# Cross-attention and mixture of experts on one core: the mixture by units of 256 rows, with the weights as stationary operand

## The reference, cut to what matters

```python
router_probs = softmax(layernorm(x) @ gate_w)          # E = 8 experts
topk_w, topk_idx = top_k(router_probs, 2)               # TOP_K = 2, weights made to sum to 1
h = silu(rows @ w1[e]) * (rows @ w3[e])                 # M = 896
out = h @ w2[e]                                         # back to D = 256
x = x + sum over the two experts of topk_w * out
```

## Time and profile before

| | us |
|---|---|
| median of the runs (462.66 to 465.39, three runs) | 465.23 |
| the profiled execution, its own time | 464.74 |
| its span | 463.0 |
| TensorE products busy (3921) | 428.7 |
| ScalarE busy | 230.9 |
| GpSimd busy | 213.3 |
| VectorE busy | 209.6 |

### The profile page before, as it was taken

How to read it: one execution, slowest core, us unless ns; L and a number is a source line. 1 busy time by engine, 2 the same in 40 slices (tenths; PEclk the granted TensorE clock), 3 DMA queues, 4 the chain that set the end, 5 groups by cost and what they waited for, 6 DMA issues and landing times.

```text
span 463.0 us, 12218 instructions
## 1 busy us (share of the span) xinstructions
PE 428.7 (93%) x3921; PEld 396.0 (86%) x3922; DVE 209.6 (45%) x582; ACT 230.9 (50%) x477; POOL 213.3 (46%) x209
## 2 busy tenths in 40 slices
PE   3899999999999999989999998999999999999970
PEld 3789988898988888979999898899999899999970
DVE  4457788758876784323233331333232333233220
ACT  3677777578865523745333732553272373333320
POOL 4424375657434641798321671482177177121121
PEclk9999999999999999999999999899999999999996
DMA  8644121462128448335731236118121121121121
GB/s 255 195 134 156 47 70 48 145 234 70 49 59 286 114 128 260 80 122 168 256 54 24 37 110 187 23 35 272 23 43 29 23 39 30 23 46 23 36 37 11
DMA packets 34523, 46.10 MB, mean 100 GB/s; under 512 B 3488, under 2 KB 29344, under 8 KB 34464
## 3 DMA queue, kind: packets, MB, share of 16 engines
q1 hardware_dynamic: 22304, 31.82, 20.6%
q0 software_dynamic: 6576, 8.82, 11.3%
q10 hardware_dynamic: 5584, 4.76, 3.7%
HBM read 32.63 MB, written 12.76 MB: 98 GB/s over the span
## 4 chain that ended last, share of the span: by engine, by line
PE 68%; DVE 9%; issue 6%; POOL 5%; DMA 4%; ACT 2%; ACTq 1%; POOLq 1%; DVEq 0%
PE bank L814 28%; PE twin L833 15%; PE bank L852 4%; DMA out_rows<-qf,x_all 3%; POOL w_lo L486 3%; PE twin L667 3%; PE bank L547 3%; PE bank L548 2%; PE bank L549 2%; DVE w_lo L1229 2%; PE bank L593 2%; PE twin L679 2%; PE bank L571 2%; PE twin L792 1%; PE bank L610 1%
## 5 line engine op out<-in xcount | busy, mean ns | idle before, releaser
L496 POOL DMA_INDIRECT out_rows<-qf,x_all x35 | 54.6, 1559 | 147.4 <-ACT qf L1054 111.7
L814 PE MATMUL bank<-w_hi,c_hi 128*128 (+1 forms) x280 | 106.4, 380 | 3.8 <-issue 2.0
L814 PE MATMUL bank<-w_lo,c_hi 128*128 (+1 forms) x280 | 103.0, 368 | 0.0
L833 PE MATMUL twin<-w_hi,kv_halves 128*128 (+1 forms) x490 | 95.2, 286 | 2.9 <-DVE kv_halves L1335 2.4
L1329 DVE TENSOR_TENSOR x_all<-bank,x_all 128x448 f32<-128x448 f32 x70 | 43.4, 623 | 97.3 <-ACT x_all L1073 97.2
L486 POOL TENSOR_TENSOR w_lo<-raw,w_hi x18 | 76.0, 4422 | 12.8 <-ACT w_hi L1066 10.1
L1335 DVE TENSOR_TENSOR kv_halves<-bank,kv_halves 128x512 fp32r<-128x512 f32 x66 | 38.6, 623 | 93.9 <-ACT kv_halves L1078 93.9
L833 PEld LDWEIGHTS twin<-w_hi,kv_halves 128*128 128x128 f32 x490 | 77.5, 188 | 3.7 <-DVE kv_halves L1335 2.6
L814 PE MATMUL bank<-w_hi,c_lo 128*128 (+1 forms) x280 | 79.9, 367 | 0.0
L1073 ACT ACTIVATE x_all<-bank 128x448 f32<-128x448 f32 x70 | 37.8, 544 | 80.6 <-PE bank L814 70.1
L833 PE MATMUL twin<-w_lo,kv_halves 128*128 (+1 forms) x245 | 68.7, 280 | 0.0
(11 more groups left out here) (219 smaller groups left out, 703.4 us busy)
## 6 DMA issues: line engine op xcount, KB each, us to landing
raw<-in_w SPq DMA_DIRECT2D x24, 896.0 KB
x_all<-bucket ACTq DMA_DIRECT2D x31, 129.0 KB, 2.1
raw<-in_ctxT SPq DMA_DIRECT2D x8, 256.0 KB, 2.9
out_rows<-x_all SPq DMA_DIRECT2D x8, 256.0 KB, 2.1
bucket<-pad_rows SPq DMA_DIRECT2D x13, 129.0 KB, 2.4
x_all<-in_x SPq DMA_DIRECT2D x2, 512.0 KB, 6.4
x_all<-bucket SPq DMA_DIRECT2D x6, 129.0 KB, 2.7
x_all<-in_x SPq DMA_DIRECT2D x1, 768.0 KB, 6.3
```

What stands on the lines that cost most here:

```text
L496: pool.indirect_dma_start(out=out, out_offset=bass.IndirectOffsetOnAxis(ap=x_in[:, v, D:D + 1].bitcast(U32), axis=0), in_=y[:, v, :], in_o ...
L814: last = nc.tensor.matmul(bank[b][:, 0:MC], stationary[:, k, :], w[:, bass.ds(at + (of + k * M + c * MC), MC)], start=(k == 0 and part == ...
L833: last = nc.tensor.matmul(bank[6][:, 0:D], stationary[:, k, :], w[:, bass.ds(at + (2 * W13 + k * D), D)], start=(k == 0 and part == 0 and ...
```

## The change

Constants: units of TWO = 256 rows instead of tiles of 128; EARLY holds two units (expert 1's and expert 0's first two tiles); a unit's last or only odd tile is a "single". The lists count units.

TensorE. The gate and up products (`gate_up`) go by blocks c of 128 of the 896 hidden columns. The weights are the stationary operand, and x, transposed, moves: 256 columns are the 256 rows of a unit. The result has the hidden columns on the partitions, as the down product needs it, so there are no transposes of g. For a single tile, x's high and low halves (`c_halves`, 2 times 128 columns) move together, and VectorE adds up the two halves of the result (`sums`); the result of low weights by low x is thereby in the sum as well.

```diff
-            def hidden(t, c):
-                for k in range(KD):
-                    for part, stationary in enumerate((x_hi, x_lo)):
-                        for b, of in ((c, 0), (2 + c, W13)):
-                            for w in ((w_hi, w_lo) if part == 0 else (w_hi,)):
-                                last = nc.tensor.matmul(bank[b][:, 0:MC], stationary[:, k, :],
-                                                        w[:, bass.ds(at + (of + k * M + c * MC), MC)], ...
+            def gate_up(t, e, c, single=False):
+                if c == 0:
+                    pe.wait_ge(x_hi_ready, t + 1)
+                    pe.wait_ge(w13_ready, e + 1)
+                if single:
+                    pe.wait_ge(summed, MB * t + max(c - 1, 0))
+                for i in range(2):
+                    if single:
+                        for k in range(KD):
+                            for w in (w_hi, w_lo):
+                                last = nc.tensor.matmul(out_ap, block(w, k), c_halves[:, :, k, 0:P], ...
+                        continue
+                    for k in range(KD):
+                        nc.tensor.matmul(out_ap, block(w_hi, k), x_hi[:, k, :], start=(k == 0), stop=False)
+                        nc.tensor.matmul(out_ap, block(w_lo, k), x_hi[:, k, :], start=False, stop=False)
+                    for k in range(KD):
+                        last = nc.tensor.matmul(out_ap, block(w_hi, k), x_lo[:, k, :], ...
+                last.then_inc(h_done, 1)
+            def down(t, c, at, tiles=2):
+                pe.wait_ge(g_lo_ready, MB * t + (c + 1))
+                for o in range(tiles):
+                    (three products: g_hi, g_lo stationary, 256 columns of w2 moving)
+            def unit(t, e, at_before, single=False):
+                gate_up(t, e, 0, single)
+                gate_up(t, e, 1, single)
+                down(t - 1, MB - 1, at_before)
+                gate_up(t, e, 2, single)
+                gate_up(t, e, 3, single)
+                first_down(t, e, tiles)
+                gate_up(t, e, 4, single)
+                down(t, 1, at, tiles)
+                x_transposes(t + 1)
+                gate_up(t, e, 5, single)
+                down(t, 2, at, tiles)
+                gate_up(t, e, 6, single)
+                for c in (3, 4, 5):
+                    down(t, c, at, tiles)
```

The early order on TensorE interleaves units 0 and 1 with the rest of the attention: rank(NPR - 1) stands behind gate_up(1, e1, 2); behind it gate_up of blocks 3 to 6 and down of blocks 0 to 4 of unit 1, then x_transposes(2), down of block 5 and the wait for six tables of the list. After that the experts are written out one by one:

```diff
+            for e in range(E):
+                of = e * NT + (3 if e < 2 else 1)
+                start = pe.value_load(tab_start[0:1, e:e + 1], ...)
+                def pairs_if_listed(j):
+                    with pe.If(pe.value_load(tab_pairs[0:1, of + 2 * j:of + 2 * j + 1], ...)):
+                        unit(start + j, e, ...)
+                        if j == 0:
+                            pairs_if_listed(1)
+                        else:
+                            with pe.If(pe.value_load(tab_pairs[0:1, of + 4:of + 5], ...)):
+                                with pe.Fori(2, NT // 2 - (1 if e < 2 else 0)) as r:
+                                    with pe.If(pe.value_load(tab_pairs[0:1, bass.ds(2 * r + of, 1)], ...)):
+                                        unit(start + r, e, e % 2 * WALL)
+                pairs_if_listed(0)
+                with pe.If(pe.value_load(tab_odd[0:1, e:e + 1], ...)):
+                    t = pe.value_load(tab_single_at[0:1, e:e + 1], ...)
+                    before_it = pe.value_load(tab_expert[0:1, bass.ds(t - 1, 1)], ...)
+                    unit(t, e, pe.snap((before_it % 2) * WALL), single=True)
```

ScalarE, VectorE and GpSimd go through the units unrolled, with tests only behind unit SURE = 16 (an untaken test leaves the whole chain of units):

```diff
+        def units_of_mixture(eng, step):
+            for t in range(AHEAD, SURE):
+                step(t)
+            def unit_if_used(t):
+                go = eng.value_load(tab_active[0:1, t:t + 1], ...)
+                with eng.If(go):
+                    step(t)
+                    if t + 1 < MOST - 2:
+                        unit_if_used(t + 1)
+            unit_if_used(SURE)
 # ScalarE
+            def silus(t, c):      (256 columns of bank c % 4, after h_done, and after summed)
+            def high_g(t, c):     (256 columns, bank to g_hi, after g_ready)
+            def mix(t):
+                high_halves(first, t, 0)
+                block_of(t, 0)
+                block_of(t, 1)
+                evacuate_y(t - 1, ...)          (two instructions of 256 columns)
+                high_halves(first, t, 1)
+                block_of(t, 2)
+                block_of(t, 3)
+                high_halves(first, t, 2)
+                block_of(t, 4)
+                block_of(t, 5)
+                evacuate_x(t + 1)               (512 columns)
+                block_of(t, 6)
+                copy_meta(t + 1)                (token numbers and weights, ring of four)
+                load(t + 2)                     (two row numbers, two DMAs)
 # VectorE
+            def products(t, c, n=TWO):  (up half of the bank times silu, back into the bank)
+            def low_g(t, c, n=TWO):
+            def sums(t, c):             (singles: 512 columns of a bank to 256, before the silu)
+            def mix(t):
+                (reads opening, single and double from the tables, three branches)
+                with dve.If(opening):
+                    for c in range(MB):
+                        if c == MB - 1:
+                            split_x(t + 1)
+                        products(t, c); low_g(t, c)
+                        if 1 <= c:
+                            low_halves(e, at, (c - 1,))
```

So the low halves of the next expert are made by VectorE, one piece of 896 columns behind each of blocks 1 to 6 of an expert's first unit (behind all blocks where the first unit is a single), and no longer by GpSimd; `w13_ready` and `w2_ready` take the place of `expert_ready`. GpSimd only adds: two adds for each unit, each after the one before, also for the empty second tile of a single:

```diff
-            def low_part(at, i):
-                return pool.tensor_tensor(w_lo[:, bass.ds(at + i * W13, W13)], ...
+            def mix(t):
+                for o in range(2):
+                    add_unit(t - 1, o)
 ...
-            pool.wait_ge(x2_stored[0], 16 * 7)
-            add(0, 0)
             scatter(NPR - 2)
             scatter(NPR - 1)
-            add(1, 1)
-            add(2, 2)
+            pool.wait_ge(x2_stored[0], 16 * 7)
+            for o in range(2):
+                add_unit(0, o)
```

More of the change, by code:

```diff
@@ L902, in _ @@
+            n = units_used(pe)
+            down(n - 1, MB - 1, (E - 1) % 2 * WALL)
         @block.scalar
@@ L1057, in high_halves @@
+            def high_halves(first, t, part):
                 if first is None:
```

676 lines of the change are left out of this document (359 added, 317 removed).

## The result

The changed kernel takes 535.35 us (median of six runs, 534.87 to 536.88), against 466.45 us for the kernel before on the same chip: a ratio of 1.150 (95% interval 1.1445 to 1.155). The forecast was 487, with a range of 464 to 505. The direction was right; the size was too small by 48 us.

What follows compares the result with a forecast made beforehand. The prediction took TensorE, busy 93% of the span, as the bound. To 464.7 us it added 11 for the first stretch, 3.5 for the middle and 7.5 for the end: 486.7, say 487, range 464 to 505 (forecast band 475 to 497).

Steps and rivals of the forecast that it cites:

- The products: TensorE's matmul work: 0.1176 us a product, 15.3 us a pair, 9.5 a single; -18.9 us in all, the only sure term.
- First stretch: Up to the start of unit 2: the longer list on VectorE delays it from 176.4 to 187, +11 us.
- The tests on TensorE: Middle stretch: loads, tests and empty rounds on TensorE's sequencer stop the array for 18.4 us, bounds 8 to 30.
- rival B: TensorE's jumps: seven untaken branches over more than one unit each fetch code, 2.65 us each, +18.6, 505 us; chance 0.22.
- The clock: Middle stretch: one wait as long as expert 2's brings TensorE a stretch at half clock, losing 1.7 us.
- The openings: Six units that prepare the next expert's weights: ScalarE's work of 18.0 us exceeds TensorE's 15.3; 3 us each, 18 in all.
- The double counting: Middle stretch: 5 us taken off for lateness of other engines made up during a test on TensorE.
- The register loads of ScalarE: Opening units: register loads, tests and DMA issues counted as 2.8 us within ScalarE's 18.0 us of work.
- The end: After the last product: two adds in a row, 4.8 us, and ScalarE's exit jump, 2.7 us; +7.5.
- Rival A: Middle stretch: waits at the handover between ScalarE, VectorE and TensorE do not appear, the work gained shows; 450 us, chance 0.16.

Runs made afterwards that it cites:

- e8_no_list: Changed kernel with every engine's order of units and the row numbers as constants, low halves on GpSimd, list of units not made: 457.14 us, ratio 0.981.
- e14_stops: e8_no_list with ten register loads in a row on TensorE ahead of the first unit of experts 2 to 7: 502.27 us, ratio 1.065.
- e4_gpsimd_low: Changed kernel with the next expert's low halves moved from VectorE back to GpSimd, in three pieces: 518.11 us, ratio 1.113.
- e1_listed: Changed kernel with TensorE's order of units as constants, no register loads or branches there; other engines keep theirs: 510.77 us, ratio 1.0965.
- e3_thin: e1_listed with the openings' pieces of the next expert's halves cut from 896 to 64 columns on ScalarE and VectorE: 478.03 us, ratio 1.028.
- e10_act_listed: Changed kernel with TensorE's and ScalarE's order of units as constants and low halves on GpSimd; VectorE and GpSimd keep their tests: 479.42 us, ratio 1.021.
- e2_short_jumps: Changed kernel with TensorE's order of units as constants but as many tests, no branch passing over a unit's code: 524.56 us, ratio 1.128.

## Why the prediction was wrong

**The products.** Right. 0.118 us each and 15.41 us for a unit without waits, against 15.3; 14 pairs and 3 singles of 9.5 make 244 us, against 242.7. The step that was called the only sure term was sure.

**First stretch.** Forecast +11, measured +13.8. The twelfth table of the list was written at 178.8 and the second x tile landed at 181.7, as the chain said (178.4 and 181.4); x's halves were complete at 184.2. TensorE's sequencer began its loads and tests at 181.8 and needed 8.4 us: 4.4 as forecast (4.3), and 4.03 for the branch at 183.6 over expert 0's pairs, which the forecast had at nothing. e8_no_list shows that the list, with the loads of row numbers, was worth 9.5 us of the time.

**The tests on TensorE, and rival B.** The loads, tests and five empty rounds were put at 18.4 us, and the far branches at nothing. From start to start of products, less the 0.118 of a product, the ten stops of the middle are 34.9 us; 14.4 of that are far branches, five of the six (the sixth lies ahead of unit 2). This was the step that failed most. I took TensorE's branch back over eight tiles (0.26 us) as the price of all its branches; six forward jumps took 2.4 to 4.0 us, because they waited for code. Rival B had the mechanism and nearly the sum, 7 x 2.65 = 18.6 us against 18.4 for six, but the sum is luck. Of the seven branches that it named only the two of experts 0 and 1 were long. The five at the third pair pass over one copy of a pair, not over more than one unit as the prediction says, and took 0.33 us each; the other four long ones are tests for a single, each close behind another jump, and the prediction did not count them. The Trainium skill ("Runtime: NRT & Kernel Launch", Instruction fetch mechanics) says that a branch out of the resident window forces a fetch; the trace agrees for the six long branches, each of which ends 1.3 to 1.4 us after a packet of q8, and a single jump over one unit's code (0.33 us, L911) did not wait for one. The prices of the loads held: the rest of the stops is 20.5 us against 18.4. (Two of that sum's items do not follow from its own 0.93 a test, 10.2 should be 10.9 and 4.0 should be 3.7, which changes it by less than 1 us.)

**The clock.** Forecast 1.7 us for one stretch, measured 14.6 in nine. The mechanism stood in the earlier trace rows and was applied to one stop only. By e14_stops each stop of 4 to 6 us costs some 2.5 us more than itself.

**The openings.** Forecast 18 us a unit, measured 18.1 to 19.8. Right in the sum, by luck, and wrong in the cause: e4_gpsimd_low shows that VectorE's pieces made them late, not ScalarE's casts. And the price hid behind TensorE's stops: without them an opening takes 19.8 (e1_listed), and the halves cost 32 us in all (e3_thin), not 18.

**The double counting.** I took off 5 us for lateness made up during a test. In the whole this was larger (removing tests gained 25 us where their stops were over 39), but it was outweighed by what was missing on the other side.

**The register loads of ScalarE.** They were in the sum of 18.0 us as 2.8 us of an engine's work, and were worth up to 18 us as e10_act_listed shows, the tests and the exit jump included, once TensorE's own stops were gone: they stand at a unit's start ahead of y, and the wait for y fell from 14.3 to 1.4 us. The sum of an engine's work does not see that.

**The end.** Forecast +7.5, measured +6.4: ScalarE's exit jump 2.97 us (2.7 forecast), the two adds 4.7 apart (4.8). The jump began 1.8 us before the last product, so only 1.7 us of it show. Its size came out near the half that was guessed; that the direction is what halves it was not tested.

**The sum.** Of the middle's 50.3 us: the work is 14 less (244 against the 258.2 of 31 tiles), the 17 us of waits of before are gone, and in their place stand 34.9 of stops at tests, 21 of waits of 0.5 to 4 us for y, g and the sums, 14.6 of half clock, and 10.5 in waits too short to list. Against the forecast's own terms, whose miss in the middle is 46.8: far branches 14.4, half clock 12.9, the shorter waits 10.5, the 5 taken off for double counting, tests 2.1, products 1.6. These are shares of the trace, not gains to be had one by one: with only the far branches gone the time fell 10 us (e2_short_jumps).

**Rival A** (450 us, the waits do not appear) had the waits wrong: they did appear. e8_no_list comes near its number, at 457.1, but with the low halves back on GpSimd and every count in the code: the change's arithmetic is a gain of some 2% over the kernel before (interval 1.4 to 2.5%), once nothing has to be looked up.

## What to carry to other kernels

Price a control-flow step by where it stands, not by how long it lasts: a register load or a test costs little where its engine waits anyway, and its full length or more where the next input of the engine that sets the rate is queued behind it. Prefer one loop over one copy of the code to nested tests over copies that may not run, keep two jumps over code that has not run from standing close behind one another, and count a long idle stretch of TensorE as itself plus the half clock behind it (each of 3.8 us and more had one here). When waits of several engines overlap, removing one shows the next: two removals together say more than either alone.

## What the runs showed of the hardware that was not expected

- A forward jump over two or three copies of a unit's code cost TensorE 3.3 and 4.0 us, a lone jump over one copy 0.33, a branch back over one unit 0.2. The second of two jumps close behind one another (L911 at 329.5, then L917 at 330.5) took 2.4 to 2.5 us, although it too passes over one unit only: it waited for the packet of code that came 1.1 us after the first. Behind a long jump it took 3.7 us.
- A stop of 4.6 us was followed by 6.1 us at a granted clock of 0.50, one of 9.1 us by 5.0 us at 0.51: the spell of half clock did not grow with the stop.
- Ten register loads in a row on TensorE took 6.5 us, of which the sequencer's lead over the array hid 2.0, as in the earlier trace rows.
